# Softmax reciprocals turned and multiplied into the value products, and a new order of a cross-attention and FFN pipeline

## The chip, the cores and the metric

The kernel runs on one core of a Trainium2 chip. The metric is the device time of one execution in microseconds (us). The time before is 826.2 us, the median of 3 runs (824.05 to 826.97).

## The reference

```python
# x [8,512,256], ctx [8,64,256], H = 16 heads, DK = 16; mask is all ones
h = layernorm(x)
Q = (h @ WQ + bQ).reshape(8, 16, -1, 16)
K, V = [(ctx @ W + c).reshape(8, 16, -1, 16) for W, c in ((WK, bK), (WV, bV))]
attn = softmax((Q @ K.T) * mask, axis=-1) / 4.0
x = x + (attn @ V).transpose(0, 2, 1, 3).reshape(8, -1, 256) @ Wp + bp
y = layernorm(x)
probs = softmax((layernorm(y) * gamma + beta) @ Wr + br)      # 8 experts
# expert 0: W1, b1, W2, b2; experts 1..7: one perturbed copy of all four, in which
# the top 5% by magnitude are shrunk by 0.8 and the bottom 5% raised by 0.8
x = x + probs[..., 0] * ffn(y, clean) + probs[..., 1:].sum(-1) * ffn(y, perturbed)
# ffn(y, w) = gelu(y @ W1 + b1) @ W2 + b2, W1 [256,1024]
```

## The kernel before, in words

Every engine has a queue written out by hand, and semaphores join them; nothing is planned by a compiler. A batch is 512 tokens by 256. A query tile j (0 to 3) has 128 queries and, for its 16 heads by 64 keys, 1024 scores. Matmuls that need full precision are done as three passes, high by high, high by low and low by high (`three`, lines 329 to 333).

After some preparation (about 67 us) there are eight **bodies**, i = 0 to 7. Body i finishes the softmax and the attention of batch i, projects it, adds the residual, normalises, computes the router's logits, and starts batch i+1 (its queries go through a DRAM scratch and come back in another layout, with the keys; then the scores of tiles 0 to 2). In between it runs the clean expert's FFN of batch i-1, in eight chunks f: `hidden` (h) makes 128 hidden features into PSUM, ScalarE makes two gelus of them (one in full precision, one rounded), GpSimd subtracts them (`low_part`), and `output` (o) adds the chunk's product to `ps_y`. Each body also advances a binary search for the weights' quantiles: a step is two `compare` pairs on VectorE (L1200), two `count` pairs on TensorE (L663), a `total` (L669) and `decide` (L1217). Bodies 0, 1, 2 and 7 have four steps, bodies 3 to 6 have three; between bodies 2 and 3 VectorE sets up the second round. After body 7 come the last clean FFN and the perturbation of the weights, and then the perturbed expert over all eight batches.

One softmax tile goes so: `scores` on TensorE (L556), `mask_scores` on VectorE (L1111, with the maximum, L1115), `shift` on GpSimd (L1008), `probs` (exp) on ScalarE (L831), `sum_probs` on VectorE (L1119, and the reciprocal L1122), `scale` on GpSimd (L1002: 128x1024 probabilities times their head's reciprocal), `turn_probs` on TensorE (L572: eight transposes), `turned` on ScalarE (L836: the copy out of PSUM), `values` on TensorE (L582: 16 small matmuls).

PSUM is four tensors of two banks each: `ps_s` (scores, values, projection), `ps_l` (turned probabilities 0 to 2, and the hidden chunks, two in turn), `ps_y` (turned probabilities 3, queries, FFN output) and `ps_m` (router, counts). TensorE's body begins:

```python
scores(i, 3); turn_probs(i, 0); turn_queries_input(i + 1)
turn_probs(i, 1); values(i, 0); count(k, 0); queries(i + 1)
values(i, 1); count(k, 1); turn_probs(i, 2); turn_probs(i, 3)
total(k); values(i, 2); h(0); values(i, 3); h(1)
```

VectorE's body begins with `sum_probs` of tiles 0 to 3, and between them tile 3's mask, the first two compares, and the low parts of the next batch's query input (L1091) and queries (L1096). Its end is: mask tile 0 of the next batch, logits, mask tile 1, low part of x2, mask tile 2, and `mix` (L1183), which adds the clean expert's result.

SyncE's queue in a body: load x and residual, `store_queries` (four transfers, L386, behind the high and the low parts), `load_queries` (two, L393, behind all four stores), `load_context` (eight of keys, L401, then mask and values). `scores(i+1, 0)` waits for the queries and the keys.

## Time and profile before

| | us |
|---|---|
| median of 3 runs | 826.2 |
| the profiled execution, whole | 828.02 |
| its span in the trace | 826.2 |
| TensorE busy | 676.4 (82%) |
| VectorE busy | 530.2 (64%) |
| ScalarE busy | 358.5 (43%) |
| GpSimd busy | 277.0 (34%) |

TensorE's mean granted clock over the span is 0.864 of full speed. A busy time counts the matmuls' modelled ends, and they overlap; a stage's length is read from the distance between starts.

### The profile page before, as it was taken

What the parts mean: (1) busy time and instruction counts of PE and PEld (TensorE: products, weight loads), DVE (VectorE), ACT (ScalarE), POOL (GpSimd) and SP (SyncE); (2) the same over time, 40 slices, a digit from 0 to 9 for tenths busy, and PEclk for the clock granted to TensorE, in tenths of its full rate; (3) what the DMA queues carried; (4) which work ended last, traced back from release to release, by engine and by line L of the source; (5) the groups of instructions that cost most, each with busy time, mean ns of one, the idle gap of its engine ahead of it and who ended that gap; (6) DMA issues with size and microseconds to landing.
All of it is one profiled execution on the core that took longest, in us unless ns stands there. A gap on an engine that the chain in (4) does not pass through costs nothing.

```text
span 826.2 us, 13556 instructions
## 1 busy us (share of the span) xinstructions
PE 676.4 (82%) x5378; PEld 561.4 (68%) x5378; DVE 530.2 (64%) x956; ACT 358.5 (43%) x512; POOL 277.0 (34%) x210
## 2 busy tenths in 40 slices
PE   5457676896898289689789779959896999999996
PEld 5345565775687268568668668848774888888884
DVE  4879579479558966856875875675499334434431
ACT  2214124445453353554545534534553444554442
POOL 2236026236244434724634643553380000000000
PEclk9657656997799589879979969959998999999999
DMA  8860512503320351341152133023020122222212
GB/s 277 150 155 4 124 52 52 123 29 92 64 72 27 102 114 38 95 104 52 55 111 65 42 93 95 26 77 103 26 77 25 52 77 76 77 77 77 64 39 51
DMA packets 133039, 64.37 MB, mean 78 GB/s; under 512 B 105712, under 2 KB 123120, under 8 KB 132976
## 3 DMA queue, kind: packets, MB, share of 16 engines
q1 hardware_dynamic: 132976, 63.51, 29.4%
q8 instruction: 42, 0.69, 0.3%
q14 instruction: 21, 0.17, 0.1%
HBM read 36.21 MB, written 23.09 MB: 72 GB/s over the span
## 4 chain that ended last, share of the span: by engine, by line
PE 55%; DVE 26%; issue 9%; POOL 5%; SPq 2%; DMA 1%; ACT 1%; DVEq 0%; ACTq 0%; POOLq 0%
PE ps_l L331 8%; PE ps_l L332 7%; PE ps_l L333 7%; PE ps_y L331 6%; PE ps_y L332 6%; PE ps_y L333 6%; DVE ind L1200 5%; POOL region_a L1002 4%; PE ps_m L663 4%; DVE region_a L1111 3%; DVE den L1119 3%; PE ps_y L572 2%; DVE acc L1183 2%; PE ps_s L582 1%; PE ps_m L613 1%
## 5 line engine op out<-in xcount | busy, mean ns | idle before, releaser
L866 ACT ACTIVATE region_b<-ps_l,bias 128x512 f32<-128x512 f32 x128 | 87.8, 686 | 171.7 <-PE ps_l L333 168.8
L1026 POOL TENSOR_TENSOR region_c_lo<-region_b,region_c_hi 128x512 fp32r<-128x512 f32 x64 | 95.2, 1497 | 109.7 <-ACT region_c_hi L869 109.7
L1200 DVE TENSOR_SCALAR ind<-key,cand 128x2048 bf16<-128x2048 uint16 x124 | 122.5, 1029 | 11.5 <-PE ps_m L663 10.6
L1455 DVE TENSOR_TENSOR region_c_lo<-region_b,region_c_hi 128x512 fp32r<-128x512 f32 x64 | 44.1, 692 | 108.2 <-ACT region_c_hi L869 108.2
L331 PE MATMUL ps_l<-x2s_hi,w_hi 128*128 128x512 f32 x256 | 109.2, 427 | 4.8 <-DVE x2s_lo L1074 4.8
L331 PE MATMUL ps_y<-region_c_hi,w_hi 128*128 128x512 f32 x256 | 102.9, 402 | 1.8 <-POOL region_c_lo L1026 1.8
L332 PE MATMUL ps_l<-x2s_lo,w_hi 128*128 128x512 f32 x256 | 103.4, 404 | 0.0
L333 PE MATMUL ps_l<-x2s_hi,w_lo 128*128 128x512 f32 x256 | 103.0, 402 | 0.0
L332 PE MATMUL ps_y<-region_c_lo,w_hi 128*128 128x512 f32 x256 | 101.3, 396 | 0.0
L333 PE MATMUL ps_y<-region_c_hi,w_lo 128*128 128x512 f32 x256 | 101.0, 394 | 0.0
L1002 POOL TENSOR_TENSOR region_a<-region_a,rs 128x1024 f32<-128x1024 f32 x32 | 65.8, 2058 | 73.6 <-DVE rs L1122 73.6
L869 ACT ACTIVATE region_c_hi<-ps_l,bias 128x512 fp32r<-128x512 f32 x128 | 87.1, 681 | 0.0
L1008 POOL TENSOR_TENSOR region_a<-region_a,mx 128x1024 f32<-128x1024 f32 x32 | 67.3, 2102 | 57.3 <-DVE mx L1115 57.2
L572 PE MATMUL ps_l<-ident,region_a 128*128 128x128 f32 x192 | 38.4, 365 | 58.5 <-POOL region_a L1002 58.5
L663 PEld LDWEIGHTS ps_m<-ones_bf,ind 128*128 128x128 bf16 x1984 | 55.8, 98 | 35.2 <-DVE ind L1200 25.9
L663 PE MATMUL ps_m<-ones_bf,ind 128*128 128x1 bf16 x1984 | 62.2, 164 | 20.1 <-DVE ind L1200 19.0
L572 PEld LDWEIGHTS ps_l<-ident,region_a 128*128 128x128 f32 x192 | 30.6, 190 | 63.5 <-POOL region_a L1002 63.5
L331 PEld LDWEIGHTS ps_l<-x2s_hi,w_hi 128*128 128x128 f32 x256 | 50.1, 196 | 19.6 <-issue 9.1
L333 PEld LDWEIGHTS ps_l<-x2s_hi,w_lo 128*128 128x128 f32 x256 | 50.0, 195 | 11.8
L332 PEld LDWEIGHTS ps_l<-x2s_lo,w_hi 128*128 128x128 f32 x256 | 50.4, 197 | 9.4
L331 PEld LDWEIGHTS ps_y<-region_c_hi,w_hi 128*128 128x128 f32 x256 | 48.3, 189 | 12.3 <-POOL region_c_lo L1026 2.6
L333 PEld LDWEIGHTS ps_y<-region_c_hi,w_lo 128*128 128x128 f32 x256 | 48.3, 189 | 11.1
(173 smaller groups left out, 1241.7 us busy)
## 6 DMA issues: line engine op xcount, KB each, us to landing
qs<-q_scr SPq DMA_DIRECT2D x16, 512.0 KB, 4.5
acc_scr<-acc SPq DMA_DIRECT2D x8, 514.0 KB, 5.0
acc<-acc_scr SPq DMA_DIRECT2D x8, 514.0 KB, 3.4
xa<-in_x SPq DMA_DIRECT2D x8, 512.0 KB, 6.2
q_scr<-qn_hi SPq DMA_DIRECT2D x16, 256.0 KB, 4.7
q_scr<-qn_lo SPq DMA_DIRECT2D x16, 256.0 KB, 5.5
x<-in_x SPq DMA_DIRECT2D x32, 128.0 KB, 4.3
xt_scr<-region_b SPq DMA_DIRECT2D x8, 512.0 KB, 2.6
```

The costliest lines, as they stand in the source:

```text
L331: eng.matmul(out_ap, a[0], b[0], start=first, stop=False)
L332: eng.matmul(out_ap, a[0], b[1], start=False, stop=False)
L333: return eng.matmul(out_ap, a[1], b[0], start=False, stop=last)
L572: mm = pe.transpose(dst[:, n // 4, (n % 4) * P:(n % 4 + 1) * P], pr[:, j % 2, n * P:(n + 1) * P], ident[:])
L663: mm = pe.matmul(ps_m[:, 1, s:s + 1], ind[s % 2][:, c * P:(c + 1) * P], ones_bf[:, 0:1], start=c == 0, stop=c == WN // P - 1)
L866: act.activation(g[:, f % 4, :], ps_l[:, f % 2, :], ACT.Gelu_apprx_tanh, bias=bias[:, e, f:f + 1]).then_inc(s["gelu"].handle, 1)
L869: act.activation(gs[0][:, f % 4, :], ps_l[:, f % 2, :], ACT.Gelu_apprx_tanh, bias=bias[:, e, f:f + 1]).then_inc(s["g_hi"].handle, 1)
L1002: pool.tensor_tensor(m, m, rs[:, j % 2, :].unsqueeze(2).to_broadcast([P, H, CT]), ALU.mult).then_inc(p_scaled.handle, 1)
L1008: pool.tensor_tensor(m, m, mx[:, j % 2, :].unsqueeze(2).to_broadcast([P, H, CT]), ALU.subtract).then_inc(s_shifted.handle, 1)
L1026: pool.tensor_tensor(gs[1][:, f % 4, :], g[:, f % 4, :], gs[0][:, f % 4, :].bitcast(F32), ALU.subtract).then_inc(s["g_lo"].handle, 1)
L1200: dve.tensor_scalar(ind[s % 2][:], key[:, key_of[rnd][s], :], cand[:, s:s + 1], None, ALU.is_le).then_inc(ind_ready.handle, 1)
L1455: dve.tensor_tensor(gs[1][:, f % 4, :], g[:, f % 4, :], gs[0][:, f % 4, :].bitcast(F32), ALU.subtract).then_inc(s["g_lo"].handle, 1)
```

## The change

1. GpSimd no longer scales the probabilities. They are turned unscaled, as soon as they are exponentiated. GpSimd instead spreads the 128x16 reciprocals to 128x256 (`spread`), TensorE turns these with two transposes (`turn_recips`), ScalarE copies them to SBUF (`keep_recips`, 128x256), and VectorE multiplies them into the value product of each tile (`divide`, 128x256, reading PSUM and writing `oTf`). The values of the tiles now go in turn through two small areas of `ps_s`.
2. PSUM is laid out anew: `ps_t` (two banks) takes all turned probabilities, the turned reciprocals, the query input, the queries and the router; `ps_h` is one bank for the hidden chunks, so that inside the bodies each `hidden` waits for both gelus of the chunk before; `ps_y` is the FFN output alone; `ps_m` is one bank. In the last clean FFN and the perturbed expert the hidden chunks use two banks in turn, as before.
3. The bodies of TensorE, ScalarE, GpSimd and VectorE are put in another order. Among others: the query input and the queries of the next batch move behind the softmax of all four tiles; `hidden` 0 moves into the softmax; the projection is split in two.

The core of the diff (left out: declarations, the same renames in the preparation, and the parts of the perturbed expert that change only their PSUM tensor):

```diff
-    ps_s, ps_l, ps_y, ps_m = (ctx.enter_context(nc.psum_tensor(f"ps_{n}", [P, 2, 512], F32)) for n in "slym")
+    ps_s, ps_t, ps_y = (ctx.enter_context(nc.psum_tensor(f"ps_{n}", [P, 2, 512], F32)) for n in "sty")
+    ps_h, ps_m = (ctx.enter_context(nc.psum_tensor(f"ps_{n}", [P, 512], F32)) for n in "hm")
+    num = [ps_s[:, n, 0:DC * P].rearrange("p (c q) -> p c q", c=DC) for n in range(2)]
+    raw = ps_t[:, 0, 0:NT * E]
...
-    turned_in = [ps_l] * (NT - 1) + [ps_y]
+    def hidden_in(e, b, f):
+
+        return ps_t[:, 0, :] if (e or b == B - 1) and f % 2 else ps_h[:]
...
 
             wait(pe, ln[0]["xhat"], b)
-            wait(pe, ex[0]["mixed"], b - 3)
+            wait(pe, inv_ready, b - 1)
...
         def turn_probs(b, j):
-            wait(pe, p_scaled, b, j + 1)
+            wait(pe, p_exp, b, j + 1)
             if j == 0:
-                wait(pe, ex[0]["g_hi"], b - 2)
-            elif j < NT - 1:
+                wait(pe, r_step, b - 1, 1)
+                if b == 0:
+                    pe.wait_ge(route_ready, 1)
+            else:
                 wait(pe, pT_ready, b, j)
-            else:
-                wait(pe, q_lo, after(b))
-                wait(pe, ex[0]["mixed"], b - 2)
-            dst = turned_in[j]
+                if j >= 2:
+                    wait(pe, inv_ready, b, j - 1)
             for n in range(G):
-                mm = pe.transpose(dst[:, n // 4, (n % 4) * P:(n % 4 + 1) * P], pr[:, j % 2, n * P:(n + 1) * P], ident[:])
+                mm = pe.transpose(ps_t[:, n // 4, (n % 4) * P:(n % 4 + 1) * P], pr[:, j % 2, n * P:(n + 1) * P], ident[:])
             mm.then_inc(p_turned.handle, 1)
+
+        def turn_recips(b, j):
+
+            wait(pe, p_spread, b, j + 1)
+            wait(pe, pT_ready, b, min(j + 2, NT))
+            if j == NT - 1:
+                wait(pe, inv_ready, b, j)
+            for c in range(DC):
+                mm = pe.transpose(ps_t[:, 0, c * P:(c + 1) * P], rsx[:, j % 2, c * P:(c + 1) * P], ident[:])
+            mm.then_inc(r_turned.handle, 1)
...
         def values(b, j):
             wait(pe, pT_ready, b, j + 1)
             if j == 0:
                 wait(pe, v_in, b)
                 wait(pe, s_masked, b)
+            elif j >= 2:
+                wait(pe, o_normed, b, j - 1)
...
-                mm = pe.matmul(ps_s[quarter:quarter + 32, n // 4, j * P:(j + 1) * P], vbd[:, n, :],
+                mm = pe.matmul(num[j % 2][quarter:quarter + 32, n // 4, :], vbd[:, n, :],
...
         def router(b):
             wait(pe, x2T_ready, b)
-            wait(pe, r_step, b - 1, 1)
+            wait(pe, q_hi, after(b))
+            wait(pe, q_lo, after(b))
+            wait(pe, inv_ready, b)
...
         def hidden(e, b, f):
             s = ex[e]
+            alone = e or b == B - 1
             if f == 0:
+                if e == 0 and b == 0:
+                    pe.wait_ge(w_lo, 2)
                 wait(pe, s["x2_hi"], b)
                 wait(pe, s["x2_lo"], b)
-                if e == 0:
-                    wait(pe, pT_ready, after(b), NT - 1)
-            if f >= 2:
-                wait(pe, s["g_hi"], b, f - 1)
-            elif e == 1:
                 wait(pe, s["g_hi"], b - 1)
+            elif f >= 2 or not alone:
+                wait(pe, s["g_hi"], b, f - 1 if alone else f)
             for c in range(DC):
-                mm = three(pe, ps_l[:, f % 2, :], [w[:, c * F + f * P:c * F + (f + 1) * P] for w in w1s],
+                mm = three(pe, hidden_in(e, b, f), [w[:, c * F + f * P:c * F + (f + 1) * P] for w in w1s],
...
         mm.then_inc(route_sum, 1)
         pe.wait_ge(proj_lo[3], 1)
         pe.wait_ge(k_lo, 1)
         scores(0, 0)
         scores(0, 1)
         scores(0, 2)
-        pe.wait_ge(route_ready, 1)
 
         def body(i, rnd, first=False, last=False):
             k = step_of(i, rnd)
-            more = i + 2 < B
+            turn_probs(i, 0)
             scores(i, 3)
-            turn_probs(i, 0)
-            if not last:
-                turn_queries_input(i + 1)
             turn_probs(i, 1)
             values(i, 0)
+            turn_recips(i, 0)
+            turn_probs(i, 2)
+            values(i, 1)
+            turn_recips(i, 1)
+            values(i, 2)
             count(k, 0)
-            if not last:
-                queries(i + 1)
-            values(i, 1)
+            turn_probs(i, 3)
             count(k, 1)
-            turn_probs(i, 2)
-            turn_probs(i, 3)
+            turn_recips(i, 2)
+            if not first:
+                hidden(0, i - 1, 0)
+            turn_recips(i, 3)
             total(k)
-            values(i, 2)
-
-
-
-            def h(f):
-                if not first:
-                    if f == 0:
-                        pe.wait_ge(w_lo, 2)
-                    hidden(0, i - 1, f)
-
-            def o(f):
-                if not first:
-                    output(0, i - 1, f)
-            h(0)
+            if not last:
+                turn_queries_input(i + 1)
             values(i, 3)
-            h(1)
             count(k + 1, 0)
-            h(2)
-            o(0)
-            project(i)
+            if not first:
+                hidden(0, i - 1, 1)
             count(k + 1, 1)
-            h(3)
+            if not last:
+                queries(i + 1, 0)
+            if not first:
+                output(0, i - 1, 0)
+                hidden(0, i - 1, 2)
+            if not last:
+                queries(i + 1, 1)
+            project(i, 0)
             total(k + 1)
-            o(1)
-            h(4)
-            o(2)
+            if not first:
+                hidden(0, i - 1, 3)
+            project(i, 1)
+            if not first:
+                hidden(0, i - 1, 4)
+                output(0, i - 1, 1)
             count(k + 2, 0)
-            h(5)
+            if not first:
+                output(0, i - 1, 2)
             count(k + 2, 1)
+            if not first:
+                hidden(0, i - 1, 5)
+            total(k + 2)
             turn_x2(i)
-            total(k + 2)
-            o(3)
+            if not first:
+                output(0, i - 1, 3)
+                hidden(0, i - 1, 6)
             if rnd == 0 or last:
                 count(k + 3, 0)
-            h(6)
+            if not last:
+                scores(i + 1, 0)
+            router(i)
+            if not first:
+                hidden(0, i - 1, 7)
             if rnd == 0 or last:
                 count(k + 3, 1)
...
+            if not first:
+                output(0, i - 1, 5)
             if not last:
                 scores(i + 1, 1)
-            o(6)
-            o(7)
...
+        def keep_recips(b, j):
+
+            wait(act, r_turned, b, j + 1)
+            wait(act, o_normed, b if j >= 2 else b - 1, j - 1 if j >= 2 else j + 3)
+            act.activation(inv[:, j % 2].rearrange("p c q -> p (c q)"), ps_t[:, 0, 0:DC * P], ACT.Copy).then_inc(inv_ready.handle, 1)
...
 
         def body(i, rnd, first=False, last=False):
             turned(i, 0)
+            turned(i, 1)
+            probs(i, 2)
+            keep_recips(i, 0)
+            turned(i, 2)
+            probs(i, 3)
+            keep_recips(i, 1)
+            turned(i, 3)
+            keep_recips(i, 2)
+            keep_recips(i, 3)
+            if not first:
+                gelu(0, i - 1, 0)
             if not last:
                 high_queries_input(i + 1)
-            probs(i, 2)
-            turned(i, 1)
+            if not first:
+                gelu(0, i - 1, 1)
+            high_output(i)
+            if not first:
+                gelu(0, i - 1, 2)
             if not last:
                 high_queries(i + 1)
-            probs(i, 3)
-            turned(i, 2)
-            turned(i, 3)
-            if not first:
-                gelu(0, i - 1, 0)
-            high_output(i)
-            if not first:
-                for f in range(1, 4):
-                    gelu(0, i - 1, f)
+            if not first:
+                gelu(0, i - 1, 3)
+            if first:
+                weights_free()
+            if not first:
+                gelu(0, i - 1, 4)
+            order_bias(i)
             normalise(1, i, x2)
-            if first:
-                act.wait_ge(w_lo, 2)
-                act.wait_ge(key_ready, 4)
-            else:
-                gelu(0, i - 1, 4)
+            if not first:
                 gelu(0, i - 1, 5)
             copy_x2(i)
             if not first:
                 gelu(0, i - 1, 6)
+            high_x2(i)
+            if not first:
                 gelu(0, i - 1, 7)
-            high_x2(i)
+            if i < DC:
+                order_bias(FC + i)
+            if not last:
+                probs(i + 1, 0)
             router_exp(i)
-            if not last:
-                probs(i + 1, 0)
-            if not first:
-                bias_y(0, i - 1)
-            if not last:
-                probs(i + 1, 1)
             if i + 2 < B:
                 normalise(0, i + 2, xa)
-            order_bias(i)
-            if i < DC:
-                order_bias(FC + i)
+            if not first:
+                bias_y(0, i - 1)
+            if not last:
+                probs(i + 1, 1)
...
+        def spread(b, j):
 
             wait(pool, p_recip, b, j + 1)
-            m = pr[:, j % 2, :].rearrange("p (h k) -> p h k", k=CT)
-            pool.tensor_tensor(m, m, rs[:, j % 2, :].unsqueeze(2).to_broadcast([P, H, CT]), ALU.mult).then_inc(p_scaled.handle, 1)
+            wait(pool, r_turned, b if j >= 2 else b - 1, j - 1 if j >= 2 else j + 3)
+            pool.tensor_copy(rsx[:, j % 2, :].rearrange("p (h d) -> p h d", d=DK),
+                             rs[:, j % 2, :].unsqueeze(2).to_broadcast([P, H, DK])).then_inc(p_spread.handle, 1)
...
         def body(i, rnd, first=False, last=False):
-            scale(i, 0)
+            spread(i, 0)
             shift(i, 3)
-            for j in range(1, NT):
-                scale(i, j)
-            if not first:
...
+                low_part(0, i - 1, 6)
             if not last:
                 shift(i + 1, 0)
-            if not first:
-                low_part(0, i - 1, FC - 1)
-            if not last:
-                shift(i + 1, 1)
             if i + 2 < B:
                 rsqrt(0, i + 2)
-            if not last:
+            if not first:
+                low_part(0, i - 1, 7)
+            if not last:
+                shift(i + 1, 1)
                 shift(i + 1, 2)
...
+        def divide(b, j):
+
+            wait(dve, o_product, b, j + 1)
+            wait(dve, inv_ready, b, j + 1)
+            if j == 0:
+                wait(dve, oT_hi, b - 1)
+                wait(dve, oT_lo, b - 1)
+            dve.tensor_tensor(oTf[:, :, j * P:(j + 1) * P], num[j % 2], inv[:, j % 2], ALU.mult).then_inc(o_normed.handle, 1)
...
         def body(i, rnd, first=False, last=False):
             k = step_of(i, rnd)
-            more = i + 2 < B
             sum_probs(i, 0)
             mask_scores(i, 3)
             sum_probs(i, 1)
+            divide(i, 0)
             compare(k, 0, rnd)
-            if not last:
-                low_queries_input(i + 1)
             sum_probs(i, 2)
             compare(k, 1, rnd)
-            if not last:
-                low_queries(i + 1)
             sum_probs(i, 3)
             counts(k)
+            divide(i, 1)
+            rank_bias(i)
             decide(k)
+            compare(k + 1, 0, rnd)
+            compare(k + 1, 1, rnd)
+            if not last:
+                low_queries_input(i + 1)
+            divide(i, 2)
+            divide(i, 3)
+            counts(k + 1)
+            low_output(i)
+            if not last:
+                low_queries(i + 1)
+            decide(k + 1)
+            if i < DC:
+                rank_bias(FC + i)
+            compare(k + 2, 0, rnd)
             if first:
-                for n in range(2):
-                    dve.tensor_copy(key[:, 2 + n, :], halfword(wraw[:, n, :], 0)).then_inc(key_ready, 1)
-            compare(k + 1, 0, rnd)
-            if not first:
-                probabilities(i - 1)
-            low_output(i)
-            compare(k + 1, 1, rnd)
-            counts(k + 1)
+                lower_keys()
             add_residual(i)
             stats(1, i, x2)
-            decide(k + 1)
-            compare(k + 2, 0, rnd)
             compare(k + 2, 1, rnd)
             counts(k + 2)
+            if not first:
+                probabilities(i - 1)
             decide(k + 2)
             if rnd == 0 or last:
-                step(k + 3, rnd)
-            if more:
-                wait(dve, x_in, i + 2)
+                compare(k + 3, 0, rnd)
+            if i + 2 < B:
                 stats(0, i + 2, xa)
+            if rnd == 0 or last:
+                compare(k + 3, 1, rnd)
             if not last:
                 mask_scores(i + 1, 0)
+            if rnd == 0 or last:
+                counts(k + 3)
+                decide(k + 3)
             logits(i)
-            rank_bias(i)
-            if i < DC:
-                rank_bias(FC + i)
             if not last:
                 mask_scores(i + 1, 1)
             low_x2(i)
@@ -1449,7 +1526,7 @@
                 split_x2(b)
```

## Rows read from the trace of the kernel before

**Rows 1.** Busy time by stretch: duration, each engine (instructions), granted clock, DMA share, GB/s

```profile
...
67.00:129.70 62.70, 42.93 (x466) 38.06 (x465) 47.62 (x93) 15.21 (x19) 21.38 (x15) 0.61 0.24 59
129.70:199.10 69.40, 57.29 (x570) 47.32 (x569) 52.12 (x100) 34.44 (x50) 33.26 (x27) 0.89 0.26 61
199.10:270.10 71.00, 59.40 (x568) 48.92 (x568) 51.14 (x98) 33.01 (x48) 31.46 (x25) 0.86 0.30 74
...
279.10:539.00 259.90, 220.75 (x2008) 184.72 (x2008) 181.53 (x343) 127.87 (x176) 124.88 (x94) 0.88 0.28 71
539.00:600.20 61.20, 51.81 (x524) 42.64 (x525) 36.37 (x74) 27.58 (x40) 24.32 (x20) 0.83 0.20 70
...
630.00:826.20 196.20, 187.48 (x832) 152.53 (x832) 76.40 (x129) 91.25 (x144) 0.00 (x0) 0.98 0.23 65
...
```

**Rows 2.** Waits of TensorE within 344 to 409 us: total, times, longest

```profile
...
PE ps_l L572 <- POOL region_a L1002: 6.5, 2, 5.5
...
```

**Rows 3.** Chain of waits in order of time, 340 to 412 us: start, duration, what

```profile
...
363.75 1.97 PE ps_y L572 x8
...
365.94 1.01 PE ps_s L582 x16
...
370.46 0.23 PE ps_l L332
...
375.42 0.12 PE ps_s L331
...
378.64 0.80 PE ps_m L663 x32
...
388.43 0.93 PE ps_s L605 x8
...
396.10 1.70 PE ps_m L613 x16
...
```

**Rows 4.** Instructions in order of time, TensorE, end of a body: start, duration

```profile
...
404.35 1.09 PE L654 MATMUL ps_y<-ident,region_b 128*128 128x128 f32 x8 [0.41 <-ACT region_b L877]
...
```

**Rows 5.** Instructions in order of time, VectorE: start, duration

```profile
...
348.69 3.51 DVE L1200 TENSOR_SCALAR ind<-key,cand 128x2048 bf16<-128x2048 uint16 x2
...
383.30 1.42 DVE L1200 TENSOR_SCALAR ind<-key,cand 128x2048 bf16<-128x2048 uint16 x2
...
408.74 1.21 DVE L1119 TENSOR_REDUCE den<-region_a 128x16 f32<-128x1024 f32 x1
...
410.16 1.22 DVE L1111 TENSOR_TENSOR region_a<-ps_s,mk 128x512 f32<-128x512 f32 x2
...
```

**Rows 6.** Instructions in order of time, ScalarE: start, duration

```profile
...
366.80 1.28 ACT L866 ACT_TABLE_LOAD   x1
369.49 0.69 ACT L866 ACTIVATE region_b<-ps_l,bias 128x512 f32<-128x512 f32 x1 [1.41 <-PE ps_l L333]
...
```

**Rows 7.** Instructions in order of time, GpSimd: start, duration

```profile
...
354.82 1.91 POOL L1002 TENSOR_TENSOR region_a<-region_a,rs 128x1024 f32<-128x1024 f32 x1 [3.17 <-DVE rs L1122]
...
403.75 2.81 POOL L1008 TENSOR_TENSOR region_a<-region_a,mx 128x1024 f32<-128x1024 f32 x1 [3.78 <-DVE mx L1115]
...
```

**Rows 8.** Transfers issued by SyncE in order of time: start, issue time

```profile
...
359.26 1.33 SPq L386 DMA_DIRECT2D q_scr<-qn_hi  x2
...
368.86 5.38 SPq L401 DMA_DIRECT2D kbd<-kh_scr  x8
...
```

**Rows 9.** Transfers that write the key tile: issue to landing

```profile
...
DMA to landing us min/median/max: 2.1/3.0/4.2
```

**Rows 10.** Stretches of 2 us around a body's start; columns as in rows 1

```profile
...
409.00:411.00 2.00, 0.00 (x0) 0.00 (x0) 1.97 (x4) 2.00 (x4) 1.34 (x2) 0.71 0.48 190
...
427.00:429.00 2.00, 1.32 (x6) 1.32 (x7) 0.00 (x0) 0.00 (x0) 0.62 (x1) 0.50 0.92 142
...
433.00:435.00 2.00, 2.00 (x21) 1.06 (x21) 0.00 (x0) 1.22 (x3) 0.00 (x0) 0.81 0.89 324
...
```

**Rows 11.** Groups by line: VectorE reading 128x256 of PSUM

```profile
...
L1288 DVE TENSOR_TENSOR region_a<-ps_s,rows 128x256 f32<-128x256 f32 x4 | 1.4, 404 | 0.0
...
```

167 lines of the change are left out of this document (93 added, 74 removed).

## The prediction

> **What bounds the kernel now.** I read the busy time by stretch first [rows 1]. The last 196.2 us, the perturbed expert, keep TensorE busy all through at a granted clock of 0.98, and the change only renames tensors there. The 29.8 us before it are VectorE's work on the weights. What can move is the 533 us of the eight bodies: 62.7 us for body 0, 69.4 and 71.0 us for bodies 1 and 2, 9.0 us between rounds, 259.9 us for bodies 3 to 6 (65.0 each) and 61.2 us for body 7. No engine is full there. In bodies 3 to 6 VectorE is busy 181.5 of 259.9 us, and the granted clock is 0.88.
>
> Then I read TensorE's waits in body 4 [rows 2]. The longest are on GpSimd's `scale`: 6.5 us in two waits, in front of the turned probabilities. The chain of waits [rows 3] gives TensorE's price of each piece without overlap. At full clock a 512-column matmul costs 0.23 us (so a chunk's h or o, six of them, costs 1.4), a 256-column one 0.12 (a projection half, 14, costs 1.7; a scores tile, eight, 0.95), a count pair 0.8, eight transposes 0.93 and the router 1.7. At half clock eight transposes cost 1.97 and a tile's values 1.01. Body 4's work by these prices is: FFN 22.6, projection 3.4, scores 3.8, turned probabilities 3.8, values 2.3, queries 2.8, counts and totals 5.3, x2, y and query turns 2.8, router 1.7, together 48.5 us. The body takes 65. So 16.5 us are waiting or half clock, nearly all in the first 26 us after the end of `turn_y` (405.44 for the next body [rows 4]), where the softmax passes round the four engines.
>
> **The change, part by part.** I walk one three-step body and count t from the end of `turn_y` (405.44).
>
> *Scaling.* Four scales of 1.9 us [rows 7] leave the path between the probabilities and their turning. Four `spread` come instead, with a quarter of the elements: between 0.2 and 1.9 us each, I take 0.6. They stand beside VectorE's sums. VectorE's compares gain too: a pair takes 3.51 us while GpSimd works and 1.42 when it doesn't [rows 5], and two pairs lie in the head; I take 2 us less each where the scales were. The Trainium skill (SBUF — State Buffer, section SBUF: two separate sides) says that VectorE in a fast mode and GpSimd hold a shared port exclusively; this trace's 3.51 against 1.42 agrees.
>
> *Added work.* TensorE: eight transposes, 0.93 to 1.97 us a body. ScalarE: four copies of 128x256; a 128x512 gelu is 0.69 [rows 6], so 0.35 to 0.69 each, I take 0.45. VectorE: four `divide`, by the PSUM group 0.40 each [rows 11], 1.6 us a body. None of these makes an engine full, but the first two stand in a chain, since every turn goes through the one `ps_t`.
>
> *The head.* Turned probabilities 0 end at t = 1.0, scores of tile 3 at 2.0. Tile 1's `shift` of 2.8 us [rows 7] ends at 1.1 as before, then probs 1, `turned` 0 (1.0 each) to 3.3, turn 1 to 4.3, `turned` 1 to 5.4. Values 0 wait for tile 3's masking, which VectorE ends at 411.4, after the first sum [rows 5], t = 6.0. They, recips 0 and its copy end at 8.1. The next turn, at half clock, ends at 10.1, `turned` 2 at 11.2, recips 1 and probs 3 and the copy by 12.7; the first count fits between. Turn 3 is over by 14.5, `turned` 3 by 15.5, recips 2 by 15.9, `hidden` 0 by 17.3, recips 3 and its copy by 18.0. VectorE reaches its fourth sum at about the same time (from the first sum at t = 3.3: four sums with their reciprocals 1.4 each, a mask with its maximum 2.4, a divide 0.4, two compare pairs of 1.4 to 3.5: 14.5 to 18.7). The head is now work of TensorE too: by t = 18 it has done all four turns, three values, a step's count and one `hidden`. Before, the first `hidden` began behind the values at 366.95 [rows 3], 26.5 us into its body (405.44 less one body of 65.0 is 340.4).
>
> *Behind the head.* ScalarE loads the gelu table (1.28) and makes the gelus of chunk 0 by t = 20.5 [rows 6]; `hidden` 1 waits for them, since it has one bank. Then come a count, queries' first half, o 0, h 2 and the second half: 28.5. Their high part follows the gelus of chunk 2 and ends at t = 29.5. From t = 28.5 to `scores(i+1, 0)` TensorE has 16.1 us of work (two projection halves 3.4, h 3 to 6 and o 1 to 3 9.9, two count pairs 1.6, the turn of x2 0.9, totals 0.3), so it is there at t = 44.6. From those scores to the end of `turn_y` it has 13.6: two more scores tiles, router, h 7, o 4 to 7, and 2.5 for the bias of y and its turn, 0.5 of it new since ScalarE now normalises first. By TensorE alone the body takes 58.2 us.
>
> *The queries' way round.* They were moved late. Before, the high part was there at 359.24 and the first store was issued at 359.26; the keys' eight transfers began at 368.86 and were issued by 374.24 [rows 8], and land 2.1 to 4.2 us after issue [rows 9]: about 17.4 us from the high part to the last key. Before, the next scores stood shortly ahead of the router, which began at 396.1 [rows 3], so some 30 us of other work covered it. Now it ends at 29.5 + 17.4 = 46.9, and `scores(i+1, 0)` stands ready at 44.6 with the router, h 7 and everything else queued behind it. It waits 2.3 us. The body takes 46.9 + 13.6 = 60.5.
>
> *Clock.* TensorE had nothing to do once the scores behind `turn_y` were through, about 406.9; the granted clock had fallen within 409 to 411 (0.71 in the mean), was at 0.5 in 427 to 429, and came back within 433 to 435 [rows 10]. After the change no idle stretch in the head is over 2 us, but many are 1 us. I add 0.8 us for a part of `hidden` at half clock: 61.3.
>
> *Sum.* Bodies 3 to 6: 4 x 61.3 = 245.2 against 259.9, saves 14.7. Bodies 1 and 2 have one step more (0.8 us before the scores, which the wait swallows, and 1.0 behind): 62.3 each, against 69.4 and 71.0, saves 15.8. Body 7 has no queries and no next scores, so no wait for keys: head 18.0, the wait for the first gelus 1.5, and behind it 15 chunks 21.2, projection 3.4, values 0.6, six count pairs 4.8, totals 0.6, turn of x2 0.9, router 1.7, bias and turn of y 2.5, together 55.2 against 61.2: saves 6.0. Body 0 has no FFN to pull forward and runs mostly at half clock (0.61 [rows 1]); VectorE's chain sets it, and I give it 2. Preparation and the last two stages: nothing. Together 39 us off the profiled 828.0: 789. The median of before lies 1.8 below that execution, so I say **788**.
>
> **The rivals.**
> 1. *Loose ends stay loose (little gain).* TensorE now has many gaps of 0.5 to 2 us in the head, each turn waiting for the copy of the one before. If the clock stays at half until t = 22, turn 3 costs 1.0 more, h 0 and h 1 1.4 each less what waits anyway: 3 us on the queries and so on the body, 64.3. Then bodies 3 to 6 save 3, bodies 1 and 2 save 10, body 7 saves 4.5: 810. For it: the same stretch was at half clock before, and body 0, sparse all through, has 0.61. Against it: the gaps are shorter than those. The Trainium skill (TensorE: Matmul & The Clock Gate, section A second HAM failure mode: psum-queue depth-cycling) tells of such a loss from small idles between groups that cycle through PSUM; nothing in this trace shows one with gaps this short.
> 2. *Better than the walk.* The keys land by t = 44.6, the clock stays up: 58.2 or less in seven bodies, 3 us less in bodies 1 to 6 and some for 0 and 7: 767. For it: the compares may all drop to 1.42.
> 3. *Slower: the queries' way round decides.* The body is the high part's time plus 31.0. It loses against 65 from t = 34 on, 4.5 us later than my walk, and against 69 to 71 from t = 39. VectorE could do this: the low part of the query input now stands behind four compare pairs, and at the contended price they cost 2.1 each more (8.4), and both halves of the queries at half clock cost 0.23 more for each of 12 matmuls (2.8). Some of that is in the walk; at 10 us late a three-step body takes 70.5 (22 us lost in four), bodies 1 and 2 71.5 (2 lost), body 0 5 more, body 7 6 less: 23 us on 826, about 849. For it: VectorE is busy 70% of these bodies already, and every compare waits for its counts. Against it: GpSimd, which makes compares dear, has 5 us less to do in the head.
> 4. *It changes nothing*: the gain and the late queries cancel, 826.
>
> **How the numbers follow.** The walk 0.45 (776 to 802), rival 2 0.20, rival 1 0.22, rival 3 0.08, rival 4 0.05. The range takes in the first three but for their outer ends: 764 to 816. About 0.3% is what a measurement of this kernel can tell from no change. Faster is 0.45 + 0.20 + 0.22 = 0.87, the same 0.05, slower 0.08.
>
> **What would show it.** Bodies 3 to 6 at 61 us each, TensorE never waiting for GpSimd before a turn, `hidden` 0 before the fourth recips, `scores(i+1, 0)` released by the transfer of the keys after a wait of 2 to 3 us, compares of 1.4 to 2 us a pair in the head. The forecast is wrong if the head still takes over 22 us to the last `keep_recips`, if the granted clock in the bodies stays under 0.88, or if the queries' high part comes later than t = 32; it is too high if the keys are never waited for.

## The result and the profile after

The changed kernel takes **803.9 us** (median of 3 runs, 803.5 to 805.1) against 826.2 before: ratio 0.974, interval 0.971 to 0.977. That is 22 us faster, and 16 us slower than the 788 forecast, inside the range of 764 to 816. A single later run of the same kernel took 796.8 beside 825.4 for the kernel before (below).

Busy time by stretch after the change; columns as in rows 1 (window and length; busy time of TensorE, its weight loads, VectorE, ScalarE and GpSimd; granted clock; share of the DMA engines; GB/s). A body runs from VectorE's first sum of its batch (`sum_probs` of tile 0) to that of the next, and t counts, as in the prediction, from the end of `turn_y`. Stretches: bodies 0, 1 and 2, the time between rounds, bodies 3, 4, 5, 6 and 7, the weights' stage, the perturbed expert.

```profile
66.99:123.71 56.72, 41.52 (x478) 35.97 (x476) 45.01 (x97) 20.32 (x31) 15.65 (x16) 0.70 0.30 75
123.71:188.44 64.73, 57.70 (x577) 48.64 (x578) 47.25 (x103) 35.56 (x53) 26.85 (x25) 0.92 0.25 57
188.44:250.90 62.46, 56.66 (x578) 46.82 (x579) 47.18 (x102) 33.91 (x49) 26.05 (x25) 0.95 0.33 84
250.90:259.54 8.64, 0.92 (x8) 0.68 (x7) 8.42 (x15) 1.02 (x1) 0.44 (x1) 0.71 0.83 243
259.54:322.30 62.76, 55.59 (x503) 46.18 (x504) 44.99 (x93) 32.88 (x48) 24.86 (x24) 0.88 0.22 50
322.30:385.07 62.77, 55.74 (x511) 46.85 (x512) 44.99 (x93) 33.75 (x49) 25.38 (x25) 0.92 0.34 84
385.07:452.05 66.98, 60.03 (x511) 50.00 (x512) 44.72 (x93) 33.78 (x49) 25.36 (x25) 0.85 0.31 79
452.05:514.80 62.75, 55.74 (x511) 46.85 (x512) 42.64 (x83) 31.81 (x45) 24.23 (x23) 0.92 0.30 75
514.80:576.30 61.50, 55.96 (x525) 45.17 (x526) 35.58 (x79) 28.26 (x41) 18.60 (x20) 0.81 0.20 70
576.30:606.00 29.70, 22.30 (x97) 16.80 (x95) 29.31 (x14) 11.05 (x18) 20.24 (x8) 0.95 0.15 53
606.00:801.70 195.70, 187.05 (x832) 151.87 (x832) 76.27 (x129) 91.30 (x144) 0.00 (x0) 0.98 0.23 65
```

Against [rows 1] 23.5 of the 24.5 us that the span lost lie in the bodies: 6.0 us in body 0, 4.7 and 8.5 in bodies 1 and 2, 4.6 in bodies 3 to 6 together (255.3 against 259.9), none in body 7 (61.5 against 61.2). TensorE's busy time is no measure of its work here: in bodies 4 and 5 it executes the same 511 matmuls and is busy 55.7 and 60.0 us, since the granted clock was 0.92 and 0.85.

The waits of TensorE in body 4, those over 1 us (total, times, longest):

```profile
PE ps_s L566 <- issue: 2.1, 1, 2.1
PE ps_s L604 <- DVE region_a L1171: 1.8, 1, 1.8
```

GpSimd's waits of [rows 2] are gone. A new one stands in the tail: the scores of the next batch, and the transfers that release them. SyncE's queue in the same body (start, issue time):

```profile
349.22 1.32 SPq L397 DMA_DIRECT2D q_scr<-qn_hi  x2
350.59 4.29 SPq L397 DMA_DIRECT2D q_scr<-qn_lo  x2
357.90 0.87 SPq L404 DMA_DIRECT2D qs<-q_scr  x2
358.81 5.93 SPq L412 DMA_DIRECT2D kbd<-kh_scr  x8
```

`turn_y` of this body ends at 320.14, so the first store is issued at t = 29.1, and the issue of the last key ends at t = 44.6. TensorE, in order of time, with the idle time before it in brackets, and below it the stretches of 3 us around it (columns as in rows 1, the granted clock third from the right):

```profile
366.40 0.35 PE L566 MATMUL ps_s<-kbd,qs 128*128 128x256 f32 x1 [2.13 <-issue]
...
367.57 3.41 PE L637 MATMUL ps_t<-gw,region_b 128*128 128x8 f32 x16
370.84 0.77 PE L340 MATMUL ps_h<-x2s_hi,w_hi 128*128 128x512 f32 x1
```

```profile
365.00:368.00 3.00, 1.60 (x11) 1.63 (x12) 0.00 (x0) 0.57 (x1) 1.27 (x1) 0.87 0.24 54
368.00:371.00 3.00, 3.00 (x16) 3.00 (x16) 1.82 (x3) 0.00 (x0) 0.00 (x0) 0.50 0.53 142
371.00:374.00 3.00, 3.00 (x8) 2.32 (x9) 2.90 (x5) 0.15 (x1) 2.23 (x2) 0.50 0.16 67
374.00:377.00 3.00, 3.00 (x16) 2.52 (x15) 0.17 (x1) 2.98 (x4) 1.70 (x3) 0.99 0.00 0
```

"issue" says only that nothing the profile shows released the matmul; the queue above names it: the last key's transfer is issued from 364.1 to 364.7, a key takes 2.2 to 4.3 us from issue to landing, and the scores start at 366.4. In bodies 0 to 6 the wait in this place is 1.4, 1.5, 0.7, 1.3, 2.1, 2.1 and 2.1 us long, and in body 0 the profile names the keys' transfer as its releaser. Behind the wait of 2.1 us the clock falls to its lower level (1.2 GHz of 2.4), the router takes 3.4 us, and the matmuls around 371 take 0.43 each against 0.23.

The head did what was hoped. TensorE, ScalarE, GpSimd and VectorE, in order of time:

```profile
325.08 0.64 PE L604 MATMUL ps_s<-region_a,vbd 128*32 128x128 f32 x16 [1.79 <-DVE region_a L1171]
...
326.66 1.94 PE L582 MATMUL ps_t<-ident,region_a 128*128 128x128 f32 x8 [0.56 <-ACT inv L877]
```

```profile
335.88 0.38 ACT L877 ACTIVATE inv<-ps_t 128x256 f32<-128x256 f32 x1 [1.24 <-PE ps_t L592]
```

```profile
323.86 0.40 POOL L1055 COPY rsx<-rs 128x256 f32<-128x256 f32 x1 [1.06 <-DVE rs L1182]
```

```profile
327.52 0.42 DVE L1191 TENSOR_TENSOR oTf<-ps_s,inv 128x256 f32<-128x256 f32 x1
327.86 1.66 DVE L1269 TENSOR_SCALAR ind<-key,cand 128x2048 bf16<-128x2048 uint16 x2
...
331.31 1.42 DVE L1269 TENSOR_SCALAR ind<-key,cand 128x2048 bf16<-128x2048 uint16 x2 [0.37 <-PE ps_m L688]
```

The spread is 0.40 in three of the four tiles and 0.86 in the other, the copy 0.38, the divide 0.42, and the two compare pairs of the head 1.66 and 1.42 against 3.51 in [rows 5].

### The profile page after: what moved, and what is told of

It is laid out like the page before. It is cut to its first block, busy times and chain, and to the rows that moved or that the text cites. A ratio compares the mean times of both kernels' runs of the same rounds, so it can differ in the third digit from the quotient of the medians.

```text
span 801.7 us, 13910 instructions
## 1 busy us (share of the span) xinstructions
PE 683.7 (85%) x5442; PEld 566.5 (71%) x5442; DVE 514.0 (64%) x988; ACT 369.3 (46%) x544; POOL 228.3 (28%) x210
## 4 chain that ended last, share of the span: by engine, by line
PE 60%; DVE 20%; issue 6%; ACT 4%; DMA 4%; SPq 3%; POOL 1%; DVEq 0%; ACTq 0%; POOLq 0%
PE ps_y L340 6%; PE ps_y L341 6%; PE ps_y L342 6%; PE ps_h L340 5%; PE ps_h L342 5%; PE ps_h L341 5%; DVE region_a L1171 3%; PE ps_t L340 3%; DVE ind L1269 3%; PE ps_m L688 3%; PE ps_t L341 3%; PE ps_t L342 3%; PE ps_t L582 3%; PE ps_t L637 2%; ACT region_a L871 2%
## 5 line engine op out<-in xcount | busy, mean ns | idle before, releaser
L907 ACT ACTIVATE region_b<-ps_h,bias 128x512 f32<-128x512 f32 x92 | 63.2, 687 | 117.9 <-PE ps_h L342 116.9
L1532 DVE TENSOR_TENSOR region_c_lo<-region_b,region_c_hi 128x512 fp32r<-128x512 f32 x64 | 44.1, 692 | 107.8 <-ACT region_c_hi L910 107.8
L340 PE MATMUL ps_h<-x2s_hi,w_hi 128*128 128x512 f32 x184 | 81.9, 445 | 5.3 <-DVE x2s_lo L1132 4.8
L342 PE MATMUL ps_h<-x2s_hi,w_lo 128*128 128x512 f32 x184 | 77.5, 421 | 0.0
L341 PE MATMUL ps_h<-x2s_lo,w_hi 128*128 128x512 f32 x184 | 77.3, 420 | 0.0
L1171 DVE TENSOR_TENSOR region_a<-ps_s,mk 128x512 f32<-128x512 f32 x64 | 40.8, 677 | 51.5 <-DMA mk<-in_mask_BxSxS_ff 35.6
L910 ACT ACTIVATE region_c_hi<-ps_h,bias 128x512 fp32r<-128x512 f32 x92 | 62.7, 681 | 0.0
L341 PEld LDWEIGHTS ps_y<-region_c_lo,w_hi 128*128 128x128 f32 x256 | 50.2, 196 | 10.4
L566 PE MATMUL ps_s<-kbd,qs 128*128 128x256 f32 x128 | 39.3, 332 | 12.7 <-issue 9.8
L866 ACT ACTIVATE region_a<-region_a 128x1024 f32<-128x1024 f32 x32 | 33.7, 1054 | 33.2 <-POOL region_a L1062 25.2
L582 PE MATMUL ps_t<-ident,region_a 128*128 128x128 f32 x256 | 41.2, 314 | 9.1 <-ACT inv L877 4.9
```

Source lines behind the costliest of these rows:

```text
L340: eng.matmul(out_ap, a[0], b[0], start=first, stop=False)
L341: eng.matmul(out_ap, a[0], b[1], start=False, stop=False)
L342: return eng.matmul(out_ap, a[1], b[0], start=False, stop=last)
L582: mm = pe.transpose(ps_t[:, n // 4, (n % 4) * P:(n % 4 + 1) * P], pr[:, j % 2, n * P:(n + 1) * P], ident[:])
L907: act.activation(g[:, f % 4, :], hidden_in(e, b, f), ACT.Gelu_apprx_tanh, bias=bias[:, e, f:f + 1]).then_inc(s["gelu"].handle, 1)
L910: act.activation(gs[0][:, f % 4, :], hidden_in(e, b, f), ACT.Gelu_apprx_tanh, bias=bias[:, e, f:f + 1]).then_inc(s["g_hi"].handle, 1)
```

## The experiments

Theories A, B and C are those that each quoted text names; A is mine in all of them. Three parts of the time are in dispute: what scaling cost, what the added turns cost, and what the late queries and keys gave back, directly and by the clock. Times below are medians; each ratio is to the kernel before, run beside it.

**1. The context first (`ctx_first`).** The keys', mask's and values' loads, the last in SyncE's queue, go in front of the stores of the queries, which don't need them:

```diff
         # SyncE's queue, body i
+                load_context(i + 1)
                 store_queries(i + 1)
                 load_queries(i + 1)
-                load_context(i + 1)
```

> The changed kernel, with the transfers of the next batch's keys, mask and values issued ahead of the stores of its queries. Theory A (the wait for the keys, and the half clock behind it, is what the bodies lose): the queries alone need about 14.3 us from their high part (8.7 to the load, 0.9 to issue, 4.7 to land) in place of 17.2, so scores of the next batch find everything there at t = 43.9; bodies 3 to 6 go from 62.8 (67.0 in body 5) to 58 to 59, the whole from 803.9 to 777 to 783. Theory B (TensorE falls to half clock behind the router's small matmuls whether it waited or not, as in body 7): only the 2.1 us of the wait go, 6 times: 790 to 794. Theory C (VectorE or another engine ends the body): under 3 us, 801 to 804.

Measured: 766.6 us (765.0 to 768.2), ratio 0.931 (0.929 to 0.933). That is 37 us less (35 by the ratios), from one call moved in one queue, and lower than any theory gave. SyncE's queue and TensorE in body 4:

```profile
317.51 6.06 SPq L412 DMA_DIRECT2D kbd<-kh_scr  x8
...
338.62 1.36 SPq L397 DMA_DIRECT2D q_scr<-qn_hi  x2
```

```profile
353.51 0.28 PE L566 MATMUL ps_s<-kbd,qs 128*128 128x256 f32 x1
...
354.47 1.85 PE L637 MATMUL ps_t<-gw,region_b 128*128 128x8 f32 x16
```

The keys are issued 21 us before the queries' first store, the scores start with no wait, and the router is at full clock again. The body takes 57.2 us against 62.8: counted from its first sum the scores start at 41.8 in place of 44.1, which is the wait, and from there to the next first sum it takes 15.4 in place of 18.7, where the clock had been at half. By the traces the span is 38.5 us shorter. The waits for the keys add up to only 11.2 of these, and 6.4 lie in body 7, which has none (55.1 us at a clock of 0.94 against 61.5 at 0.81). Body 3 gains only 1.8 us: its head is at half clock in both kernels.

**2. The keys later still (`keys_late`).** The opposite push: the eight key transfers go behind the mask and the values (in short; comments stand for the calls):

```diff
+            # mask, 4 transfers; values, 2
             wait(sp, s_product, b - 1)
             # keys, 8 transfers
-            # mask, 4 transfers; values, 2
```

> The changed kernel, with the keys' eight transfers issued behind the mask's four and the values' two, so 4.2 us later in every body. Theory A: each of bodies 0 to 6 takes 4.2 us more, and somewhat more where a longer idle time costs more clock: 803.9 + 29 to 36, so 833 to 840, slower than the kernel before. Theory C (something else ends the body at about the same time): under 10 us more.

Measured: 835.4 us (two runs, 834.0 and 836.9), ratio 1.014 (1.012 to 1.016); slower than the kernel before, and within theory A's 833 to 840. In body 5:

```profile
464.84 0.55 PE L566 MATMUL ps_s<-kbd,qs 128*128 128x256 f32 x1 [5.70 <-issue]
```

The wait grows by 3.6 us, bodies 3 to 6 take 68.0 us in the mean against 63.8, and the order of one queue decides between 767 and 835. Body 7, behind all these waits, is 5.6 us shorter than in the changed kernel (55.9 against 61.5), so a long wait in the bodies before it does not by itself bring body 7 its half clock.

**3. The context first in the old kernel (`before_ctx`).** The same edit as in 1, in the kernel before.

> The kernel before with the keys, the mask and the values issued ahead of the stores of the queries. There the keys landed some 15 us before they were needed, so by theory A nothing moves: 822 to 826. If the order of the transfers is worth something by itself (queries' stores, x and residual sharing the engines): beyond 3 us either way.

Measured: 826.1 us (823.7 to 826.8), ratio 1.000 (0.999 to 1.001). There the way round lay under 30 us of other work. The values' load now holds up the queue behind it, so that the queries' first store leaves 10 us later in body 4 (369.4 in place of 359.3), and even that costs nothing. The late keys are a cost that the change brought in.

**4. The wait filled (`fill_wait`).** The wait stays, TensorE's idleness goes: nine 512-column products into `ps_t`, which nobody reads, in front of `scores(i+1, 0)` in bodies 1 to 6.

```diff
+                wait(pe, q_hi, i + 1)
+                wait(pe, q_lo, i + 1)
+                wait(pe, inv_ready, i)
+                for n in range(9):
+                    pe.matmul(ps_t[:, 0, :], w1s[0][:, 0:P], w1s[0][:, 0:S], start=True, stop=True)
                 scores(i + 1, 0)
```

> The changed kernel, with nine 512-column matmuls (2.1 us at full clock, into the query area of PSUM, their result is not used) in front of the first scores of the next batch, in bodies 1 to 6: they fill the wait for the keys and don't shorten it. If idleness costs the clock behind the wait (3.5 us of the 5.6 by which a body with the keys first is shorter): bodies 3 to 6 go from 62.8 (67.0) to 59 to 60, the whole from 803.9 to 783 to 792. If the half clock comes from the router's small matmuls: no gain, 802 to 806, the 2.1 us of filling hidden in the wait. If the filling comes too late or too long: slower by up to 2 a body.

Measured: 788.2 us (784.9 to 792.2), ratio 0.957 (0.953 to 0.960). Body 4, TensorE:

```profile
360.41 2.23 PE L806 MATMUL ps_t<-w_hi 128*128 128x512 f32 x9
362.88 0.36 PE L566 MATMUL ps_s<-kbd,qs 128*128 128x256 f32 x1 [0.24 <-issue]
...
363.90 1.85 PE L637 MATMUL ps_t<-gw,region_b 128*128 128x8 f32 x16
```

Useless work in place of idleness is worth 16 us in the medians (9 against the later run of the changed kernel, experiment 8). In body 4 the scores even start 1.8 us later (45.9 us behind the first sum against 44.1), but the router behind them takes 1.85 us instead of 3.41, and the rest of the body 16.2 in place of 18.7. More of the gain lies elsewhere: body 5 takes 59.3 against 67.0, and body 7, which has no fill, 55.1 at 0.94 against 61.5 at 0.81; body 6 takes 1.5 more (64.3). Half clock in one body thus hangs on more than its own instructions: on what ran before it, or on where in time its gaps fall. No run tells these two apart. Idleness in front of the scores was a cause of it; how the 37 us of experiment 1 split exactly into wait and clock, this run doesn't tell.

**5. No scaling in the old kernel (`before_noscale`).** The kernel before without GpSimd's `scale`; the outputs lack the softmax's normalisation. `probs` then also waits for the sums of the tile whose buffer it overwrites (not shown).

```diff
         def turn_probs(b, j):
-            wait(pe, p_scaled, b, j + 1)
+            wait(pe, p_exp, b, j + 1)
...
-            scale(i, 0)
-            for j in range(1, NT):
-                scale(i, j)
```

> The kernel before in its old order, with the scaling of the probabilities left out (the output is not normalised): turning waits for the exponential. It tells the share of the scaling from that of the order. If the scaling on the path is most of the gain: 826.2 - 25 to 35, so 791 to 801, since each of the four scales (1.9 us) and the dear compares (2 us each) go. If the order is most of it: under 12 us, 814 to 826.

Measured: 774.1 us (772.1 to 776.6), ratio 0.940 (0.938 to 0.942). Bodies 3 to 6 take 58.1 us each against 65.0, at a clock of 0.93 against 0.88, and body 0 takes 57.6 against 62.7. So the scaling held 52 us (50 by the ratio), clock included, more than both theories gave.

**6. No reciprocals in the new kernel (`no_recips`).** `spread`, `turn_recips` and `keep_recips` go, and `divide` multiplies by 1.0; again the outputs lack the normalisation. This takes the added work away, in the changed kernel with its late keys.

```diff
-            turn_recips(i, 0)      # and 1, 2, 3; keep_recips and spread as well
...
-            dve.tensor_tensor(oTf[:, :, j * P:(j + 1) * P], num[j % 2], inv[:, j % 2], ALU.mult).then_inc(o_normed.handle, 1)
+            dve.tensor_scalar(oTf[:, :, j * P:(j + 1) * P], num[j % 2], 1.0, None, ALU.mult).then_inc(o_normed.handle, 1)
```

> The changed kernel without the spreading, turning and copying of the reciprocals (the value products are multiplied by 1.0 and the output is not normalised). It prices the added work. By the head of body 4 each turned pair with its copy stands for 0.8 to 1.3 us in the chain through the one PSUM tensor, four in a body: bodies 2 to 4 us shorter in the head, but the queries' way round moves with it: 803.9 - 15 to 28, so 776 to 789. If VectorE's sums and masks end the head anyway: 800 to 804.

Measured: 789.5 us (788.6 to 793.6), ratio 0.959 (0.957 to 0.962). 14 us less by the medians and 10 by the spans, half a microsecond above what the theory gave. Of these 8.9 lie in body 7 (52.6 us at 0.94 against 61.5 at 0.81) and 5.2 in body 5; bodies 1 to 3 are 1.3 to 2.9 us longer, with longer waits for the keys (2.4 in place of 1.3 us in body 3). Where the keys are late, work taken out of the head is hardly gained.

**7. The same with the context first (`ctx_no_recips`).** Edits 1 and 6 together, without the normalisation, so that the keys hide nothing.

> Keys first, and no spreading, turning and copying of the reciprocals (the output is not normalised): the new order without the added work and without the wait for the keys. Against the kernel with keys first (766.6) it prices the added work: by the chain through the one PSUM tensor 2 to 3 us a body, 745 to 757. If VectorE's masks and sums set the head: 762 to 767. Against the old order without scaling (774.1) it prices the new order alone.

Measured: 757.6 us (756.5 to 758.9), ratio 0.918 (0.916 to 0.920). Against 766.6 the added turns cost 9 us in all, about 1.1 a body where the theory had 2 to 3, just above its 757. They don't cost it evenly: by the traces, in which the span is 6.6 us shorter, body 3 gains 4.2, bodies 4 to 6 gain 0.4 to 1.3, and body 7 takes 1.9 more. Against 774.1 of experiment 5, which has no normalisation either, the new order with the banks of its own and the early context is worth 17, after the four `divide` that it still does.

**8. The changed kernel again (`after_again`).**

> The kernel after once more, unchanged, for its trace alone. In the first trace body 5 took 67.0 us where bodies 3 and 4 took 62.8, and body 7 61.7 where 55.4 was seen in ctx_first. Theory A (these come out of the order of the work, which is the same every time): body 5 is 66 to 68 and body 7 61 to 62.5 again, each with the same stretches at half clock. Theory B (they come out of where the clock's changes happen to fall): some other body is the long one, and body 7 is anywhere from 55 to 62; the total is within 803 to 806 in either case.

Measured: 796.8 us in its one run, 7 less than the median above. Bodies 5 and 7 are the long ones again:

```profile
378.00:445.60 67.60, 60.82 (x511) 50.55 (x512) 44.33 (x93) 33.78 (x49) 25.35 (x25) 0.82 0.31 78
...
508.16:569.65 61.49, 55.95 (x525) 45.18 (x526) 35.69 (x79) 28.28 (x41) 18.61 (x20) 0.81 0.20 70
```

These two bodies are as long as in the first trace, so their half clock is repeatable. The total lay outside 803 to 806: bodies 0 to 2 were 5.9 us shorter in sum. The kernel's own time varies by about 1% between sessions, more than its three runs beside each other showed. A difference to its 803.9 is thus good to some 7 us, unless the bodies in the traces show it too; the 37 of experiment 1 is well outside, while the 16 of experiment 4 and the 14 of experiment 6 would be 9 and 7 against this run.

**9. Filled heads (`ctx_warm`).** `ctx_first` with seven 512-column products a body where TensorE waits for the softmax, into `ps_h`, read by nobody. The edit puts the five behind the second turn of the probabilities and the two behind the first turn of the reciprocals, not at the places that the text below names:

```diff
             turn_probs(i, 1)
+            fill(i, 5)
             values(i, 0)
             turn_recips(i, 0)
+            fill(i, 2)
             turn_probs(i, 2)
```

> ctx_first with filling products added in every body: five 512-column products behind the first turn of the probabilities' head part and two behind the last turn, into the feed-forward's own bank, which nothing reads. They take 7 x 0.21 to 0.43 us of TensorE where it waits for VectorE and GpSimd. ctx_first measured 766.6. Theory A (idle stretches of TensorE are what costs its clock): the bodies of ctx_first still show half clock in their heads (first three bodies above all), the filling takes some of it away, and the time is 755 to 763. Theory B (in ctx_first the clock is no longer on the path that sets the end; VectorE sets the heads): 766 to 769. Theory C (the fillings stand in the way of turns): 770 or more.

Measured: 755.7 us (755.3 to 764.3), ratio 0.919 (0.913 to 0.924), **the fastest complete kernel** here. Bodies 3, 4 and 7:

```profile
248.10:306.00 57.90, 52.10 (x504) 43.97 (x504) 44.97 (x92) 32.78 (x48) 24.84 (x24) 0.94 0.24 54
306.00:362.50 56.50, 52.80 (x517) 44.37 (x517) 44.90 (x93) 33.69 (x49) 25.79 (x25) 1.00 0.38 93
...
475.45:528.26 52.81, 48.24 (x532) 39.53 (x533) 35.93 (x79) 28.29 (x41) 19.01 (x20) 1.00 0.23 81
```

The clock is 1.00 throughout bodies 4 to 7. The gain lies where `ctx_first` had a clock below 1: 2.4, 1.2 and 3.0 us in bodies 0, 1 and 3 (0.69, 0.92 and 0.86), 0.7 and 0.8 in bodies 4 and 5 (0.97 both), 2.3 in body 7 (0.94). Bodies 2 and 6, at 1.00 already, and the perturbed expert (195.2 us in both) gain nothing. The two kernels ran in different sessions; by their ratios the difference is 10 us.

**10. Filled heads with the late keys (`after_warm`).** The same edit in the changed kernel.

> The kernel after with filling products in every body's head (five of 512 columns behind the second turn of the probabilities, two behind the first turn of the reciprocals, into the feed-forward's bank, read by nobody); the late keys stay. The same edit took ctx_first from 766.6 to 755.7. Theory A (the half clock in the last body and the longer body 5 come from the idle stretches of their own heads): the last body goes from 61.7 to 55 to 57, body 5 from 67 to about 63, and the time to 780 to 792. Theory B (they come from the wait for the keys in the body before, carried on): the last body stays at 61 to 62, and the time is 798 to 806.

Measured: 788.9 us (782.7 to 793.4), ratio 0.954 (0.947 to 0.960), inside theory A's range. Bodies 4 to 7 take 59.0, 58.5, 62.4 and 59.5 us: body 5 is shorter than A had it, and the last body, at a clock of 0.86, lies between the two theories. TensorE in bodies 4 and 6:

```profile
367.22 0.36 PE L566 MATMUL ps_s<-kbd,qs 128*128 128x256 f32 x1 [1.48 <-issue]
...
368.24 1.85 PE L637 MATMUL ps_t<-gw,region_b 128*128 128x8 f32 x16
...
485.76 0.35 PE L566 MATMUL ps_s<-kbd,qs 128*128 128x256 f32 x1 [2.59 <-issue]
...
486.79 2.36 PE L637 MATMUL ps_t<-gw,region_b 128*128 128x8 f32 x16
```

After a wait of 1.5 us the clock stayed up (1.00 in every stretch of the body), after 2.6 us it fell. Body 6 takes 3.4 us more than body 4, of which 1.1 is wait and 2.3 come behind it.

**11. The last body's head alone (`warm_last`).**

```diff
+            if i == B - 1:
+                fill(i, 5)      # and fill(i, 2), as in 9
```

> The kernel after with the same filling in the head of the last body alone. That body has no keys to load for another, so it has no wait for keys of its own; in the two traces of the kernel after it took 61.7 and 61.8 us at a granted clock of 0.81. Theory A (its own head's idle stretches cost it the clock): it takes 55 to 57 us at 0.93 or more, all others are as before, and the time is 5 to 7 us under the 796.8 to 803.9 of the kernel after. Theory B: it stays at 61 to 62 us and the time does not change.

Measured: 797.1 us (789.4 to 800.9), ratio 0.964 (0.958 to 0.970); by the total neither theory is told from the other, since the kernel itself lies anywhere from 796.8 to 803.9. The trace tells: body 7 takes 58.0 us at 0.88, against 61.5 at 0.81 in both traces of the changed kernel, which is between the two theories.

```profile
513.80:571.80 58.00, 53.66 (x532) 43.57 (x533) 35.45 (x80) 28.29 (x41) 18.89 (x20) 0.88 0.21 74
```

So with its head filled body 7 is 3.5 us shorter. The rest of its half clock comes later, at two places that are half clock here too, and stays open.

## Why the prediction was right and wrong

**Right in sign and mechanism.** By the stretches, the profiled execution (803.5 us) is 14 us over the walk's 789: body 0 4.0 under, bodies 1 and 2 2.6 over, bodies 3 to 6 10.1 over, body 7 6.3 over, the remainder 1 under. The 4.0 of body 0 hid a part of the miss by luck. The granted clock of bodies 3 to 6 rose only from 0.88 to 0.89 in the mean; below 0.88 the prediction would have called itself wrong.

**The head.** Forecast: last `keep_recips` at t = 18.0. Measured: it ends at 336.26, t = 16.1. The assumed 0.6 for `spread` was 0.40 in most tiles, 0.45 for the copy 0.38, 0.40 for the divide 0.42, and the compares came down to 1.66 and 1.42, at the low end of 1.4 to 3.5. GpSimd is never waited for ahead of a turn of the probabilities. One turn (326.66, 1.94 us) was at half clock.

**The queries.** Forecast: high part at t = 29.5, keys landed and scores started at 46.9, TensorE ready at 44.6, a wait of 2.3. Measured: 29.1, 46.3, 44.1, 2.1. Of the 1.9 us that the head came early, 0.4 were left by the high part; waits for the query input (0.7 and 0.4) took a part. This is the term that the forecast had best, and experiments 1 to 3 show it to be the right one: without the wait 37 us go, with a longer one 32 come, and the old kernel doesn't care.

**The step that failed is the clock.** The walk added 0.8 us a body, "for a part of `hidden` at half clock", in the head, and took the tail, from the scores to the end of `turn_y`, at full clock: 13.6. The pieces that it lists there add up to 13.2, or 14.1 with the first scores tile; the same stretch takes 13.4 in `ctx_first`, at full clock, so the size of the work was right. In the changed kernel it measured 16.5, as the wait of 2.1 us was followed by about 6 us at half clock. The forecast priced the wait as 2.3 us; it cost 5.6 in body 4 (experiment 1), and experiment 4 shows that idleness was a cause of it. Body 5 lost still more (67.0 us; `ctx_first` 57.3), and body 7, which has no wait for keys, missed most: forecast 55.2 by full clock, measured 61.5 at 0.81. With the head filled and no late keys the same body takes 52.8 at 1.00, so the sum of its work was 2.4 too high and the clock cost more than the miss of 6.3 shows.

The prediction said of gaps this short that nothing in the trace of before showed a loss by them. The traces of after do: in body 4 the clock is 1.00 until 326, gaps of 1.79 and 0.56 us stand before the turn of 1.94 us, and filling gaps of this size took 11 us off `ctx_first`. The Trainium skill (TensorE: Matmul & The Clock Gate, section A second HAM failure mode: psum-queue depth-cycling) tells of such a loss from small idles; these rows agree in that, but the longer gap here is a wait for VectorE's masking and not for PSUM. Nor do the gaps decide it alone. In body 7 of `fill_wait`, whose head has no fill, the same turn behind the same gaps stayed at full clock:

```profile
505.42 0.65 PE L604 MATMUL ps_s<-region_a,vbd 128*32 128x128 f32 x16 [1.74 <-DVE region_a L1177]
...
507.00 1.07 PE L582 MATMUL ps_t<-ident,region_a 128*128 128x128 f32 x8 [0.56 <-ACT inv L883]
```

**The rivals.** Rival 1 (810; its own savings of 3, 10 and 4.5 give 809) had the right kind of loss but at the wrong place: it put the half clock into the first 22 us, and in body 4 the larger part sat behind the wait for the keys. Rival 2's state (keys in time, clock up: 58.2 us a body, 767) is `ctx_first` to the microsecond in the total, 766.6, with bodies 4 to 7 at 57.2, 57.3, 56.5 and 55.1. That the totals meet so closely is luck: body 3 is at 61.0, and body 0, at 55.7, is 5 us under the walk. Rival 3's mechanism, the queries' way round, is real and was at work; `keys_late`, where the keys and not the queries come later, shows it past its point of decision, slower at 835. Body 0, given 2 us on no more than an estimate, gained 6.0; 5.1 of these come in the old kernel too when the scaling alone goes (experiment 5).

**What scaling cost.** The gain in sight was larger than the walk had it. In round numbers from experiments 1, 5 and 7: 826 less 52 (scaling gone) less 17 (order, banks, context early) plus 9 (turned reciprocals) gives 766, and the late keys put 37 back. The change realised 22 of 60 us; one call moved in a queue brings the rest.

## What to carry to other kernels

When work is moved later, follow what it releases through every queue behind it: the keys' loads did not depend on the queries, but stood behind their stores, and so inherited their lateness. Price a wait of TensorE not by its length alone but by the matmuls behind it at half clock, which in body 4 more than doubled it. Where a short wait can't be removed, try filling it with matmuls into a bank that nobody reads: in `fill_wait` that paid although the scores of body 4 started 1.8 us later. A loss by the clock may show in another body than the one where the wait stands, so compare all of them.

## What the runs showed of the hardware

**The clock fell while TensorE was busy.** In body 7 of the changed kernel, TensorE in order of time, and the 3-us stretches around it (columns as in rows 1):

```profile
558.29 0.95 PE L688 MATMUL ps_m<-ones_bf,ind 128*128 128x1 bf16 x32
559.11 1.93 PE L637 MATMUL ps_t<-gw,region_b 128*128 128x8 f32 x16
560.90 0.48 PE L340 MATMUL ps_h<-x2s_hi,w_hi 128*128 128x512 f32 x1
```

```profile
557.00:560.00 3.00, 3.00 (x47) 2.56 (x46) 1.11 (x2) 1.27 (x2) 0.96 (x2) 1.00 0.43 175
560.00:563.00 3.00, 3.00 (x19) 2.24 (x19) 1.46 (x2) 0.00 (x0) 1.43 (x1) 0.80 0.01 3
563.00:566.00 3.00, 3.00 (x38) 2.58 (x38) 0.16 (x1) 2.82 (x4) 0.55 (x1) 0.50 0.02 5
```

There is no idle time, busy is 3.00 of 3.00, and yet the clock goes from 1.00 to 0.50 after 32 one-column and 16 eight-column products. In `ctx_warm` the same sequence left it at 1.00, and so it did in body 7 of `fill_wait`, which has no fill of its own. What came before, or where in time the sequence fell, counts too; which of it does is open.

**The length of a wait did not tell what followed.** In body 4 of `after_warm` a wait of 1.48 us left the clock alone; in body 3 of the changed kernel 1.27 us, in the same place, brought it down, as 2.13 and 2.59 did elsewhere:

```profile
303.67 0.36 PE L566 MATMUL ps_s<-kbd,qs 128*128 128x256 f32 x1 [1.27 <-issue]
```

```profile
306.00:309.00 3.00, 3.00 (x11) 2.61 (x11) 1.47 (x3) 0.00 (x0) 0.00 (x0) 0.50 0.66 197
```

And two bodies with the same instructions and the same wait (2.13 and 2.09 us) took 62.8 and 67.0 us, repeatably.

**Useless matmuls shortened the kernel.** 56 added products took 11 us off `ctx_first`, and the nine of each of six bodies 16 us off the changed kernel (9 against its later run).
